# Attention's extra work spread over the steps, with two PSUM banks for row maxima and the division moved to GpSimd

## The chip, the cores and the metric

The kernel runs on one core of one Trainium2 chip. The metric is the device time of one execution in microseconds (us). Engines are named as in the profile: PE is TensorE, DVE is VectorE, ACT is ScalarE, POOL is GpSimd, SP issues most DMAs.

## What is computed

A chain of four blocks on x of shape (16, 64, 32, 32): a transformer block, a residual block of two 3x3 convolutions, an iterative whitening, and a state-space block. Only the attention of the first block is touched. It works on 16 images of 1024 positions, with 8 heads of 32 channels:

```python
x_ln = layer_norm(x_flat, g1, beta1)
qkv = x_ln @ w_qkv.T
q, k, v = jnp.split(qkv, 3, axis=-1)
scores = jnp.einsum('bhqd,bhkd->bhqk', q, k) * HEAD_DIM ** (-0.5)
attn = jax.nn.softmax(scores, axis=-1)
out = jnp.einsum('bhqk,bhkd->bhqd', attn, v)
```

All of it is float32 in the kernel, apart from bfloat16 copies of Q and K that serve only to find each row's maximum.

## The kernel before

Each phase of the kernel is a block of five instruction streams, one per engine, with semaphores between them. `attention_phase` takes the images one after another and the heads in two groups of four (`GH`), so there are 32 groups (`NG`). A group is one call of `period` in each engine's stream: 16 steps (`STEPS`), 8 for each half of 512 queries, each step one block of 128 keys. The first and the last group have stages of their own, a `lead` period runs ahead of the first, and the loop in `image_loop` covers four groups an iteration (two images), seven times.

In a step PE makes the transposed scores of four heads (`scores`, L398, one bank of `at_sc` each; a head uses 32 rows of the array) and takes off the maxima by a matmul with one row (`at_nrow`, L401). ACT takes the exponential of heads 0 and 1, then of heads 2 and 3 (L479), into `at_probs`; the scores of the next step wait for `exp_done` of the pair whose banks they use. PE multiplies the step before's `at_probs` by V (`values`, L410) into the bank `at_O`.

Beside this, the row maxima of the next group are made: in each step four matmuls of Q by K in bfloat16 (`maxima`, L334; heads 0 and 1 behind the scores, heads 2 and 3 at the step's end), each into one bank of `at_ring`, and DVE reduces each bank to 128 numbers (L526). `LATE` says how many of these maxima slip into the next period. Half of them are gathered by `combine`, turned by four matmuls with the identity (`turn`, L372) and copied by ACT into `at_nrow`.

The table `extra` puts the rest of the work in the steps: Q and K projections (`project`, L347, a matmul of 64 rows; ACT copies each to `at_QT` or `at_KT`, DVE casts it from the same bank to `at_QH` or `at_KH`, L542), V (`values_projected`, L360), the turns, and the softmax denominators (`denominators`, L385). POOL adds up five of the eight blocks of `at_probs` in four sums (L580); PE multiplies ones by the other three blocks and by that sum, which makes four terms of four heads into one bank. ACT makes the reciprocal of it as exp(-ln) in `at_lden` and `at_rden`, and DVE multiplies `at_O` by it (`normalise`, L549) into `at_att`, which SP stores. Values of a new half wait for that (`od_free`).

Maxima and extras share the three banks of `at_ring` in turn: `period_units` numbers them in the order in which PE issues them and gives each the number modulo `SLOTS`. `wait_for_bank` lets PE wait until the unit before it in the same bank was read, and for a projection also until it was cast.

## Time and profile before

| | us |
|---|---|
| median of 3 runs | 4073.43 (4072.83 to 4073.93) |
| the profiled execution | 4079.2 |
| its span, first to last instruction | 4077.5 |
| first exponential of attention (L479) starts | at 103.5 |
| last exponential of attention starts | at 2111.4 |
| busy: PE, DVE, ACT, POOL | 3426.7, 2982.9, 2143.2, 2103.6 |

Attention takes about half of the span. Everything is read from one profiled execution; its own time stands beside its span, and it is a little above the median of the runs. Busy time of PE counts matmuls whose ends are modelled, so starts are the better thing to read.

### The profile page before, as it was taken

The numbers are of one execution on the slowest core, as the hardware profiler recorded it, in microseconds if no ns is written. First come the engines' busy times: TensorE is split into PE (matmuls) and PEld (weight loads), VectorE is DVE, ScalarE is ACT, GpSimd is POOL, SyncE is SP. The second block draws the span as 40 slices with busy tenths as digits, with TensorE's granted clock in tenths as the row PEclk, the third lists the DMA queues.
The fourth block names the chain that finished last, engine by engine and source line by source line (L and its number), as shares of the span: only waits on it lengthen the run. The fifth ranks groups of instructions, "written<-read, shape, count | busy, mean of one in ns | idle before, by whom it ended". The sixth has DMA issues, their size and how long they took to land. (4 is left out here: it accounts for less than half of the span.)

```text
span 4077.5 us, 56384 instructions
## 1 busy us (share of the span) xinstructions
PE 3426.7 (84%) x19376; PEld 1233.0 (30%) x19376; DVE 2982.9 (73%) x3235; ACT 2143.2 (53%) x2331; POOL 2103.6 (52%) x586
## 2 busy tenths in 40 slices
PE   6999999999999999999978996567777777767766
PEld 2333333333333333333322333222222222222222
DVE  5677677676776767767722221489999999999999
ACT  3566566565665656656543332255555554555554
POOL 0556556565565555655660000156665666656665
PEclk7999999999999999999998998778888888888888
DMA  2000000000000000000013111200000000000000
GB/s 93 11 14 17 10 14 17 15 14 14 10 17 15 14 15 12 14 15 14 12 39 111 67 36 54 102 9 8 9 12 8 10 8 8 13 8 10 8 8 8
DMA packets 34702, 90.68 MB, mean 22 GB/s; under 512 B 8304, under 2 KB 9396, under 8 KB 34356
## 3 DMA queue, kind: packets, MB, share of 16 engines
q1 hardware_dynamic: 29396, 70.53, 5.6%
q0 software_dynamic: 5056, 16.83, 1.1%
q8 instruction: 155, 2.54, 0.3%
q14 instruction: 95, 0.78, 0.1%
HBM read 49.03 MB, written 38.27 MB: 21 GB/s over the span
## 5 line engine op out<-in xcount | busy, mean ns | idle before, releaser
L526 DVE TENSOR_REDUCE at_pmax<-at_ring 128x1 f32<-128x512 f32 x2048 | 1305.1, 685 | 511.4 <-PE at_ring L334 510.8
L479 ACT ACTIVATE at_probs<-at_sc 128x1024 f32<-128x1024 f32 x1024 | 992.5, 1021 | 659.6 <-PE at_sc L401 659.5
L1623 POOL TENSOR_TENSOR ss_drive<-ss_du,ss_bsb 128x1024 f32<-128x1024 f32 x261 | 865.2, 3333 | 392.4 <-ACT ss_bsb L1469 312.9
L580 POOL TENSOR_TENSOR at_prob_sums<-at_prob_sums,at_probs 128x2048 f32<-128x2048 f32 x192 | 869.4, 4528 | 109.8 <-ACT at_probs L479 98.7
L398 PE MATMUL at_sc<-at_QT,at_KT 32*128 32x512 f32 x4096 | 848.2, 643 | 21.3 <-issue 20.9
L1560 DVE TENSOR_TENSOR_SCAN ss_state<-ss_decay,ss_drive 128x1024 f32<-128x1024 f32 x259 | 774.7, 2991 | 7.5 <-ACT ss_decay L1476 5.1
L580 POOL TENSOR_TENSOR at_prob_sums<-at_probs 128x2048 f32<-128x2048 f32 x64 | 291.0, 4547 | 789.9 <-ACT at_probs L479 789.9
L1377 PE MATMUL ss_Y<-ss_seen,ss_ident 128*128 128x512 f32 x1032 | 598.3, 710 | 58.7 <-DVE ss_yv L1577 58.7
L410 PE MATMUL at_O<-at_probs,at_V 128*32 128x512 f32 x4096 | 538.9, 610 | 53.0 <-DVE at_att L549 51.8
L1469 ACT ACTIVATE ss_bsb<-ss_B 128x1024 f32<-128x1024 f32 x262 | 268.3, 1024 | 537.1 <-PE ss_B L1359 535.9
L334 PE MATMUL at_ring<-at_KH,at_QH 32*128 32x512 bf16 x2048 | 447.3, 389 | 5.7 <-DVE at_pmax L526 2.9
L1359 PE MATMUL ss_C<-ss_bc,ss_select 96*128 96x512 bf16 x518 | 175.5, 424 | 298.3 <-DVE ss_seen L1568 298.2
L401 PE MATMUL at_sc<-at_nrow,at_ones_bf 1*128 1x512 bf16 x2048 | 339.6, 381 | 0.0
L398 PEld LDWEIGHTS at_sc<-at_QT,at_KT 32*128 32x128 f32 x4096 | 275.1, 186 | 175.6 <-ACT at_probs L479 149.2
L1377 PEld LDWEIGHTS ss_Y<-ss_seen,ss_ident 128*128 128x128 f32 x1032 | 229.8, 227 | 315.0 <-issue 220.4
L1568 DVE TENSOR_TENSOR ss_seen<-ss_state,ss_C 128x1024 f32<-128x1024 f32 x259 | 316.2, 1221 | 9.5 <-DVE ss_state L1560 0.7
L334 PEld LDWEIGHTS at_ring<-at_KH,at_QH 32*128 32x128 bf16 x2048 | 150.9, 92 | 534.0 <-DVE at_pmax L526 343.0
L1476 ACT ACTIVATE ss_decay<-ss_delta,ss_a 128x1024 f32<-128x1024 f32 x261 | 297.4, 1140 | 2.9 <-DVE ss_delta L1544 2.9
L938 POOL DMA_DIRECT2D scratch_x<-fc_out x8 | 4.3, 536 | 351.5 <-ACT fc_out L839 351.5
L1359 PE MATMUL ss_B<-ss_bc,ss_select 96*128 96x512 bf16 x524 | 168.5, 405 | 13.3 <-ACT ss_bsb L1469 7.8
L385 PE MATMUL at_ring<-at_probs,at_ones 128*32 128x512 f32 x1512 | 175.3, 596 | 1.4 <-DVE at_pmax L526 1.4
L410 PEld LDWEIGHTS at_O<-at_probs,at_V 128*32 128x32 f32 x4096 | 87.5, 108 | 273.0 <-issue 189.1
(192 smaller groups left out, 2846.2 us busy)
## 6 DMA issues: line engine op xcount, KB each, us to landing
scratch_attn<-at_att SPq DMA_DIRECT2D x64, 256.0 KB, 2.0
fc_att<-scratch_attn SPq DMA_DIRECT2D x32, 512.0 KB, 5.8
at_xn<-scratch_xn SPq DMA_DIRECT2D x32, 256.0 KB, 3.8
ss_xn<-scratch_xm SPq DMA_DIRECT2D x17, 256.0 KB, 3.5
ss_xw<-scratch_xw SPq DMA_DIRECT2D x17, 256.0 KB, 3.4
ln_x<-in_x SPq DMA_DIRECT2D x8, 512.0 KB, 4.8
scratch_xn<-ln_xn POOLq DMA_DIRECT2D x8, 512.0 KB, 3.0
fc_x<-in_x SPq DMA_DIRECT2D x8, 512.0 KB, 7.7
```

Of the source, the lines that this page charges most:

```text
L334: nc.tensor.matmul(ring[:, unit[3], :], QH[head(h), p, blk(quad // 2)], KH[head(h), p, hs(quad % 2)], start=True, stop=True).then_inc(max_ ...
L398: nc.tensor.matmul(sc[:, h, :], KT[head(h), par, blk(kb)], QT[head(h), par, hs(half)], start=True, stop=False)
L401: m = nc.tensor.matmul(sc[:, h, :], ones_bf[row, :], nrow[row, half, :], start=False, stop=True)
L410: m = nc.tensor.matmul(O[head(h), :], V[:, par, kb, head(h)], probs[:, kb, h, :], start=(kb == 0), stop=(kb == KB - 1))
L479: nc.scalar.activation(probs[:, kb, two, :].rearrange("p h q -> p (h q)"), sc[:, two, :].rearrange("p h q -> p (h q)"), ACT.Exp, scale=SCA ...
L526: nc.vector.tensor_reduce(pmax[:, quad // 2, h, quad % 2:quad % 2 + 1], ring[:, unit[3], :], AX_X, ALU.max, negate=True).then_inc(max_done, 1)
L580: nc.gpsimd.tensor_tensor(prob_sums[:, half, :, :], before, probs[:, k, :, :], ALU.add).then_inc(pool_sums, 1)
L1359: m = nc.tensor.matmul(dst[:, hs(h)], select[:, first + n, :], bc[0:3 * 2 * N, par, hs(h)], start=True, stop=True)
L1377: m = nc.tensor.matmul(Y[:, hs(h)], ident[:], seen[:, n % DEPTH, hs(h)], start=(n == 0), stop=(n == N - 1))
L1560: nc.vector.tensor_tensor_scan(state[:, n % 2, :], decay[:, n % DEPTH, :], drive[:, n % DEPTH, :], 0.0, ALU.mult, ALU.add).then_inc(state_ ...
L1568: nc.vector.tensor_tensor(seen[:, n % DEPTH, :], state[:, n % 2, :], Cp[:], ALU.mult).then_inc(seen_done, 1)
L1623: nc.gpsimd.tensor_tensor(drive[:, n % DEPTH, :], du[:, par, :], bsb[:, n % DEPTH, :], ALU.mult).then_inc(drive_done, 1)
```

## The change

`LATE` goes from 3 to 5. Maxima get two banks, heads 0 and 2 the first and heads 1 and 3 the second; every extra goes to the third. The extras have one kind a step: Q, K, Q, K in steps 0 to 3, the turns in 6 and 14, V in halves in 7 and 8. The denominators of the second half of the group before are made in steps 4 and 5, two terms each, those of the first half in steps 10 to 13, one term each (`den_terms`), and values follow in every step. DVE casts a projection at the start of the next step. ACT copies `at_O` to the new tile `at_raw` (`take_out`) when a half's values are done; that frees `at_O`, and POOL multiplies the copy by the reciprocal after its sums of a half, under a new semaphore `att_done` that SP's store and ACT's next reciprocal wait for.

```diff
-    LATE = 3
+    LATE = 5
...
-    extra = {0: [("q", 0), ("k", 0)], 1: [("q", 1), ("k", 1), ("den", 1)], 4: [("turn", 1)], 6: [("v", 0), ("v", 1)],
-             9: [("den", 0)], 12: [("turn", 0)]}
+    extra = {0: [("q", 0)], 1: [("k", 0)], 2: [("q", 1)], 3: [("k", 1)], 5: [("den", 1)], 6: [("turn", 1)],
+             7: [("v", 0)], 8: [("v", 1)], 13: [("den", 0)], 14: [("turn", 0)]}
+
+    den_terms = {4: (1, (0, 1)), 5: (1, (2, 3)), 10: (0, (0,)), 11: (0, (1,)), 12: (0, (2,)), 13: (0, (3,))}
...
-        found, at = [], 0
+        found = []
         for s in range(STEPS):
-            plan = [("max", h) for h in (0, 1)] + extra.get(s, []) + [("max", h) for h in (2, 3)]
-            for kind, which in plan:
-                if executed(stage, kind, which, s):
-                    found.append((s, kind, which, at % SLOTS))
-                at += 1
+            plan = [("max", h) for h in range(GH)] + extra.get(s, [])
+            found += [(s, kind, which, which % 2 if kind == "max" else 2) for kind, which in plan
+                      if executed(stage, kind, which, s)]
...
                 srcs = [probs[:, k, :, :] for k in range(SUMMED + 1, KB)] + [prob_sums[:, half, :, :]]
-                for n, src in enumerate(srcs):
+                for n in terms:
+                    if n == 0:
+                        wait_for_bank(stage, grp, unit)
+                    if n == len(srcs) - 1:
+                        pe.wait_ge(pool_sums, SUMMED * (2 * (grp - half) + half + 1))
                     for h in range(GH):
-                        m = nc.tensor.matmul(ring[head(h), unit[3], :], ones[:, head(h)], src[:, h, :],
+                        m = nc.tensor.matmul(ring[head(h), unit[3], :], ones[:, head(h)], srcs[n][:, h, :],
                                              start=(n == 0), stop=(n == len(srcs) - 1))
...
+                    for kind, which in extra.get(s, []):
+                        if kind in "qk":
+                            project(stage, grp, par, kind, which)
+                        elif kind == "v":
+                            values_projected(stage, grp, par, which)
+                        elif kind == "turn":
+                            turn(stage, grp, which)
                     if stage != "lead":
-                        if s == 0:
-                            if stage != "first":
-                                values(grp - 1, 1 - par, STEPS - 1)
-                        elif s % KB == 2:
-                            values(grp, par, s - 2)
-                            values(grp, par, s - 1)
-                        elif s % KB != 1:
-                            values(grp, par, s - 1)
+                        if s in den_terms:
+                            denominators(stage, grp, *den_terms[s])
+                        if s:
+                            values(grp, par, s - 1)
+                        elif stage != "first":
+                            values(grp - 1, 1 - par, STEPS - 1)
...
+            def take_out(grp, half):
+
+                act.wait_ge(pv_done, STEPS * grp + KB * (half + 1))
+                if not (isinstance(grp, int) and grp == 0):
+                    act.wait_ge(att_done, 2 * grp + half - 1)
+                nc.scalar.activation(raw[:, half, :], O[:], ACT.Copy).then_inc(od_free, 1)
...
-                    if s == 2 and stage not in ("lead", "first"):
-                        normalise(grp - 1, 1)
-                    if s == KB + 2 and stage != "lead":
-                        normalise(grp, 0)
+                    for kind, which in extra.get(s - 1, []):
+                        if kind in "qk":
+                            cast(stage, grp, par, kind, which)
                     reduce(stage, grp, s, (0, 1))
-                    if s < 2:
-                        cast(stage, grp, par, s)
                     reduce(stage, grp, s, (2, 3))
...
         def _(pool):
+            def normalise(grp, half):
+                pool.wait_ge(rden_done, 2 * grp + half + 1)
+                pool.wait_ge(od_free, 2 * grp + half + 1)
+                if not (isinstance(grp, int) and grp == 0):
+                    pool.wait_ge(att_stored[half], grp * DMA)
+                nc.gpsimd.tensor_tensor(att[:, half, :], rden[:], raw[:, half, :], ALU.mult).then_inc(att_done, 1)
...
+                    if not (stage == "first" and half == 0):
+                        normalise(grp - 1 + half, 1 - half)
```

The order on PE around the denominators of the first half. Before, in step 9 (`at_ring<-at_KH,at_QH` is a matmul for maxima, `at_ring<-at_probs,at_ones` one for denominators, `at_sc` the scores):

```order
L334 MATMUL at_ring<-at_KH,at_QH 128x512 [waits at_max_done] x2
L385 MATMUL at_ring<-at_probs,at_ones 32x512 [waits at_pool_sums,at_max_done]
L385 MATMUL at_ring<-at_probs,at_ones 32x512 x11
L385 MATMUL at_ring<-at_prob_sums,at_ones 32x512 x4
L334 MATMUL at_ring<-at_KH,at_QH 128x512 [waits at_max_done] x2
L398 MATMUL at_sc<-at_QT,at_KT 128x512 [waits at_exp_done]
L398 MATMUL at_sc<-at_QT,at_KT 128x512
L398 MATMUL at_sc<-at_QT,at_KT 128x512 [waits at_exp_done]
L398 MATMUL at_sc<-at_QT,at_KT 128x512
L401 MATMUL at_sc<-at_nrow,at_ones_bf 128x512 x4
L334 MATMUL at_ring<-at_KH,at_QH 128x512 [waits at_extra_done]
L334 MATMUL at_ring<-at_KH,at_QH 128x512 [waits at_max_done]
```

Now, steps 10 and 11, from the maxima of heads 2 and 3 on:

```order
L335 MATMUL at_ring<-at_KH,at_QH 128x512 [waits at_max_done] x2
L385 MATMUL at_ring<-at_probs,at_ones 32x512 x4
L411 MATMUL at_O<-at_probs,at_V 32x512 x4
L335 MATMUL at_ring<-at_KH,at_QH 128x512 [waits at_max_done] x2
L399 MATMUL at_sc<-at_QT,at_KT 128x512 [waits at_exp_done]
L399 MATMUL at_sc<-at_QT,at_KT 128x512
L399 MATMUL at_sc<-at_QT,at_KT 128x512 [waits at_exp_done]
L399 MATMUL at_sc<-at_QT,at_KT 128x512
L402 MATMUL at_sc<-at_nrow,at_ones_bf 128x512 x4
L335 MATMUL at_ring<-at_KH,at_QH 128x512 [waits at_max_done] x2
```

All sixteen denominator matmuls stood together, and no values with them; now four stand ahead of the values of each step, between the maxima of heads 0 and 1 and those of heads 2 and 3.

The order on DVE in steps 0 to 3, where projections are cast. Before, from ahead of step 0's first cast (the rows of `at_pmax` are the reductions of the maxima):

```order
L526 TENSOR_REDUCE at_pmax<-at_ring 128x1 [waits at_max_ready] x22
L542 CAST at_QH<-at_ring 128x512 [waits at_extra_done]
L542 CAST at_KH<-at_ring 128x512 [waits at_extra_done]
L526 TENSOR_REDUCE at_pmax<-at_ring 128x1 [waits at_max_ready] x4
L542 CAST at_QH<-at_ring 128x512 [waits at_extra_done]
L542 CAST at_KH<-at_ring 128x512 [waits at_extra_done]
L526 TENSOR_REDUCE at_pmax<-at_ring 128x1 [waits at_max_ready] x6
L534 TENSOR_REDUCE at_negm<-at_pmax 128x16 [waits at_max_done]
```

Now:

```order
L534 TENSOR_REDUCE at_pmax<-at_ring 128x1 [waits at_max_ready] x16
L550 CAST at_QH<-at_ring 128x512 [waits at_extra_done]
L534 TENSOR_REDUCE at_pmax<-at_ring 128x1 [waits at_max_ready] x4
L550 CAST at_KH<-at_ring 128x512 [waits at_extra_done]
L534 TENSOR_REDUCE at_pmax<-at_ring 128x1 [waits at_max_ready] x4
L550 CAST at_QH<-at_ring 128x512 [waits at_extra_done]
L534 TENSOR_REDUCE at_pmax<-at_ring 128x1 [waits at_max_ready] x4
L550 CAST at_KH<-at_ring 128x512 [waits at_extra_done]
L534 TENSOR_REDUCE at_pmax<-at_ring 128x1 [waits at_max_ready] x4
L542 TENSOR_REDUCE at_negm<-at_pmax 128x16 [waits at_max_done]
```

Casts came in pairs between a step's second and third reduction; now there is one behind each step's fourth. DVE's multiplication into `at_att` is gone.

## Rows read from the trace of the kernel before

**Rows 1.** the page: busy time of each engine, two groups of POOL (busy us, mean ns)
```profile
PE 3426.7 (84%) x19376; PEld 1233.0 (30%) x19376; DVE 2982.9 (73%) x3235; ACT 2143.2 (53%) x2331; POOL 2103.6 (52%) x586
...
L1623 POOL TENSOR_TENSOR ss_drive<-ss_du,ss_bsb 128x1024 f32<-128x1024 f32 x261 | 865.2, 3333 | 392.4 <-ACT ss_bsb L1469 312.9
L580 POOL TENSOR_TENSOR at_prob_sums<-at_prob_sums,at_probs 128x2048 f32<-128x2048 f32 x192 | 869.4, 4528 | 109.8 <-ACT at_probs L479 98.7
```

**Rows 2.** windows: stretch and its us, then per engine busy us (instructions), PEclk, DMA
```profile
1050.14:1111.60 61.46, 58.85 (x483) 20.90 (x480) 44.59 (x72) 37.37 (x45) 36.24 (x8) 1.00 0.03 10
1238.59:1302.52 63.93, 61.46 (x484) 21.52 (x480) 44.86 (x72) 37.58 (x44) 36.27 (x8) 0.95 0.06 18
1238.59:1245.50 6.91, 6.91 (x30) 2.34 (x28) 3.91 (x6) 3.13 (x4) 0.00 (x0) 0.53 0.00 0
```

**Rows 3.** timeline at the loop's end: start, us, engine, line, instructions [idle before <-releaser]
```profile
1236.06 2.24 PE L398 MATMUL at_sc<-at_QT,at_KT 32*128 32x512 f32 x8 [3.26 <-issue]
...
1245.73 1.02 ACT L479 ACTIVATE at_probs<-at_sc 128x1024 f32<-128x1024 f32 x1 [3.27 <-PE at_sc L401]
```

**Rows 4.** timeline of ACT in the group from 1173.05
```profile
1173.05 1.94 ACT L479 ACTIVATE at_probs<-at_sc 128x1024 f32<-128x1024 f32 x2 [1.24 <-PE at_sc L401]
...
1177.72 1.94 ACT L479 ACTIVATE at_probs<-at_sc 128x1024 f32<-128x1024 f32 x2 [1.76 <-PE at_sc L401]
...
1188.94 1.94 ACT L479 ACTIVATE at_probs<-at_sc 128x1024 f32<-128x1024 f32 x2 [2.31 <-PE at_sc L401]
...
1198.48 1.94 ACT L479 ACTIVATE at_probs<-at_sc 128x1024 f32<-128x1024 f32 x2 [1.24 <-PE at_sc L401]
...
1206.12 1.94 ACT L479 ACTIVATE at_probs<-at_sc 128x1024 f32<-128x1024 f32 x2 [1.24 <-PE at_sc L401]
1209.30 1.94 ACT L479 ACTIVATE at_probs<-at_sc 128x1024 f32<-128x1024 f32 x2 [1.24 <-PE at_sc L401]
...
1218.59 1.94 ACT L479 ACTIVATE at_probs<-at_sc 128x1024 f32<-128x1024 f32 x2 [2.31 <-PE at_sc L401]
```

**Rows 5.** timeline of PE in a plain step
```profile
1206.20 1.07 PE L410 MATMUL at_O<-at_probs,at_V 128*32 128x512 f32 x8
...
1207.20 0.39 PE L334 MATMUL at_ring<-at_KH,at_QH 32*128 32x512 bf16 x2
```

**Rows 6.** timeline of step 10
```profile
1215.35 1.92 PE L410 MATMUL at_O<-at_probs,at_V 128*32 128x512 f32 x16 [0.82 <-DVE at_att L549]
...
1217.20 0.39 PE L334 MATMUL at_ring<-at_KH,at_QH 32*128 32x512 bf16 x2
...
1217.21 1.24 PE L398 MATMUL at_sc<-at_QT,at_KT 32*128 32x512 f32 x8
1217.63 1.29 DVE L526 TENSOR_REDUCE at_pmax<-at_ring 128x1 f32<-128x512 f32 x2 [1.14 <-PE at_ring L334]
...
1218.39 0.38 PE L334 MATMUL at_ring<-at_KH,at_QH 32*128 32x512 bf16 x2
...
1218.70 1.07 PE L410 MATMUL at_O<-at_probs,at_V 128*32 128x512 f32 x8
```

**Rows 7.** timeline of step 0
```profile
1173.28 1.29 DVE L526 TENSOR_REDUCE at_pmax<-at_ring 128x1 f32<-128x512 f32 x2 [0.61 <-PE at_ring L334]
1174.02 0.29 PEld L347 LDWEIGHTS at_ring<-at_xn,at_w 64*128 64x128 f32 x2 [0.59 <-DVE at_pmax L526]
1174.87 0.60 ACT L461 ACTIVATE at_QT<-at_ring 128x512 f32<-128x512 f32 x1
...
1175.08 1.06 PE L410 MATMUL at_O<-at_probs,at_V 128*32 128x512 f32 x8
...
1175.51 0.69 DVE L542 CAST at_QH<-at_ring 128x512 bf16<-128x512 f32 x1 [0.94 <-ACT at_QT L461]
```

**Rows 8.** timeline of step 6, PE
```profile
1199.46 1.16 PE L360 MATMUL at_ring<-at_w,at_xn 64*128 64x128 f32 x16 [0.82 <-DVE at_pmax L526]
```

**Rows 9.** timeline of step 4, PE
```profile
1192.20 0.40 PE L372 MATMUL at_ring<-at_ident,at_negm 128*128 128x128 bf16 x4
```

More of the change, by code:

```diff
@@ L284, in store @@
             def store(b, g, half):
-                sp.wait_ge(od_free, 2 * (GROUPS * b + g) + half + 1)
+                sp.wait_ge(att_done, 2 * (GROUPS * b + g) + half + 1)
                 sp.dma_start(attn_d[bass.ds(b, 1), g * P:(g + 1) * P, hs(half)].rearrange("a c s -> (a c) s"),
@@ L350, in values_projected @@
-            def values_projected(stage, grp, par):
-                if not executed(stage, "v", 0, 6):
-                    return
-                units = [unit_of(stage, "v", n) for n in range(2)]
-                for unit in units:
-                    wait_for_bank(stage, grp, unit)
-                at = 2 * INNER + (1 - par) * P
-                for k in range(KB):
-                    n = k % 2
-                    rows = slice(n * C, (n + 1) * C)
-                    m = nc.tensor.matmul(ring[:, units[n][3], blk(k // 2)], xn[rows, blk(k)], w[rows, at:at + P],
+                unit = unit_of(stage, kind, half)
@@ new lines, in project, with values_projected @@
+                wait_for_bank(stage, grp, unit)
+                n = "qk".index(kind)
+                rows = slice(n * C, (n + 1) * C)
+                at = n * INNER + (1 - par) * P
+                nc.tensor.matmul(ring[:, unit[3], :], w[rows, at:at + P], xn[rows, hs(half)],
+                                 start=True, stop=True).then_inc(extra_ready, 1)
+            def values_projected(stage, grp, par, n):
+                if not executed(stage, "v", n, 0):
+                    return
+                unit = unit_of(stage, "v", n)
+                wait_for_bank(stage, grp, unit)
+                at = 2 * INNER + (1 - par) * P
+                for j in range(KB // 2):
+                    rows = slice(n * C, (n + 1) * C)
+                    m = nc.tensor.matmul(ring[:, unit[3], blk(j)], xn[rows, blk(2 * j + n)], w[rows, at:at + P],
@@ L374, in turn, with denominators @@
                 m.then_inc(extra_ready, 1)
-            def denominators(stage, grp, half):
+            def denominators(stage, grp, half, terms):
                 if not executed(stage, "den", half, 0):
@@ L481, in period @@
                                                  scale=SCALE).then_inc(exp_done, 1)
+                    if kb == 0 and stage not in ("lead", "first") or stage == "first" and s == KB:
+                        take_out(grp - 1 + half, 1 - half)
                     for kind, which in extra.get(s, []):
```

61 lines of the change are left out of this document (21 added, 40 removed).

## The prediction, made before the change was timed

> **What bounds the kernel now.** I first read the page [rows 1]: TensorE is busy 84% of the span and no other engine is above 73%. The page's queue and DMA lines show nothing near full, so I went to one attention group. The windows view cut at group boundaries [rows 2] gives 61.46 us for a plain group, with TensorE busy 58.85 of it (96%) and granted its full clock; DVE is busy 44.59, ACT 37.37 and POOL 36.24. Attention is 32 such groups and only it is changed. One boundary in four (the loop's end) costs more: TensorE idles 3.26 us without a releaser [rows 3], and the group behind it takes 63.93 at a mean granted clock of 0.95 [rows 2]. Nothing in the change touches that.
>
> The ACT timeline of a group [rows 4] gives its steps: a step is the time from one pair of exponentials to the next. A step with nothing extra takes 3.18 us (1209.30 - 1206.12). Step 0 takes 4.67, 1.49 more; steps 1 and 2 together 11.22, 4.86 more; steps 6 and 7 together 7.64, 1.28 more (V); steps 9 and 10 together 9.29, 2.93 more. That is 10.56, and with 16 x 3.18 the group. These lumps are what the change spreads out.
>
> **A plain step** is a loop of two engines [rows 4, 5]: ACT works 1.94, then idles 1.24 until the scores are back, because heads 2 and 3 wait for the second exponential. **A step full of TensorE work** runs differently [rows 6], step 10 with two `values` of four heads: values start at 1215.35, max matmuls of heads 2 and 3 at 1217.20 with the scores of all four heads right behind (the exponentials were long done), the exponential at 1218.59 [rows 4], the next values at 1218.70. So from the max matmuls M to the next exponential is 1.39, to the next full-array work 1.50, and a step without waits is 3.35 with two values. From one set of values to M is 1.00 (1206.20 to 1207.20), from two sets 1.85: one set costs 0.85, and so does a denominator term, which has the same shape. A step with only its own values would be 3.35 - 0.85 = 2.50 of work: 0.68 of each plain step is free.
>
> **The change, part by part**, for a middle group; X is the extra TensorE work of a step.
> - Denominators: four terms as one burst (steps 1, 9) become two terms in steps 4 and 5, and one each in 10 to 13. Same matmuls; X = 1.70 or 0.85.
> - Projections: Q and K in steps 0 and 1 become one each in steps 0 to 3. The K matmul starts at 1174.02 and values follow at 1175.08 [rows 7]: X = 1.05. The two V halves, 1.16 together [rows 8], now go one a step, each on 64 of the array's rows. The bounds are 0.58 and 1.16; I take 1.0, since on different rows the two halves most likely ran side by side, as the heads' scores do.
> - Turns: X = 0.40 [rows 9], in steps 6 and 14.
> - Output: DVE's two multiplications leave (0.69 each, by its cast of the same shape [rows 7]); ACT adds a copy of 0.60 (as its Q copy [rows 7]) after the values of steps 0 and 8, POOL a multiplication. The values at the start of a half no longer wait for a reciprocal (0.82 at 1215.35 [rows 6]). For POOL's price the bounds are DVE's 0.69 and half of its own 128x1024 multiply, 3.33 / 2 = 1.67 [rows 1]; I take 1.2, a quarter of its 4.53 for 128x2048 [rows 1] plus a little. POOL is idle 25 us of a group [rows 2]. Its four sums of half 0 (18.1 us from step 1) end in step 5, and the reciprocal of step 13 asks for that product much later, so it costs nothing in the loop; if POOL were full, ACT's reciprocal would wait for `att_done` with every exponential behind it. The Trainium skill (GPSIMD Engine Reference, section 4.1) says to keep elementwise work of two inputs on VectorE since GpSimd takes about twice as long. My 1.2 against 0.69 agrees with that. Were the difference on the path in each of 64 halves, it would be +33 us, 4183; by the rows POOL has room and it is 0.
> - ACT in step 0: values end about 2.4 after the step's start, copy 0.6, Q 0.6: 3.6 to 3.9, under the 4.02 below. Close, but hidden; the same in step 8. If its cover went, each would cost its excess over the step. SP's stores wait for `att_done` and nothing waits for SP.
>
> **The banks are the price.** Maxima now have two banks, so head 1's max matmul of a step needs the reduction of head 3 of the step before; with three banks it needed head 2's. Heads 2 and 3 are issued at M = 1217.20 [rows 6], DVE starts at 1217.63, needs 1.29 for both (done at M + 1.71), and the release takes about 0.05 (1173.28 + 0.69 to 1174.02 [rows 7]): head 1 can start at M + 1.77. Before, it started at M + 1.19 (1218.39), on time. TensorE works in order, so extras and values stand behind it, and from such a matmul to full-array work is 0.31 (1218.39 to 1218.70). So they start at M + 2.07, not M + 1.50. To the next M is X + 1.00 (values 1206.20, M 1207.20 [rows 5]). **A step in a row of full steps takes 3.07 + X**; in place of 2.50 + X. The DVE work that was free is now inside the chain.
>
> In steps 1 to 4 there is more: the third bank holds one extra at a time, released by DVE's cast, which stands behind head 3's reduction. Reductions start 0.61 apart (1.29 for two, the last 0.69): cast at M + 0.42 + 1.22, done 0.69 later, released M + 2.38. Steps 1 to 3 take 2.38 + 1.05 + 1.00 = 4.43.
>
> The sum of a group, each step in us: step 0 4.02 (behind a plain step whose M is 1.69 after its exponential: M + 1.77 is 0.27 into step 0, + 0.31 + 1.05 + 1.00 + 1.39); 1 to 3 13.29; 4 2.38 + 1.70 + 1.00 = 5.08; 5 4.77; 6 3.47; 7 and 8 8.14; 9 3.18 (its chain needs only 3.07); 10 3.82; 11 to 13 11.76; 14 3.47; 15 3.18. Total 64.18 against 61.46: **+2.72 per middle group, 30 groups: +82.** It is a gain of 10.56, all lumps gone, and a loss of 13.3 in new ones.
>
> At the ends: the first group has no steps 4/5 denominators (about -1.5 by the same table); the last has no projections, and two more steps of maxima are hidden in it: about 4 less; copy and POOL's product add 1 at the end; the lead-in reduces 8 maxima fewer (-5) and loses as much to cast chains and to two banks at half clock. Together -5, from rows only roughly. The profiled execution (4079.2, span 4077.5) gives 4079 + 77 = 4156; it is 5.8 above the median of the runs, 4073.43, to which I apply the sum: **4150**.
>
> **Rivals.**
> A, faster: the banks never delay TensorE. It needs M to head 1's matmul to last 1.77 by itself, as when heads 2 and 3 still wait for the exponential [rows 4, 5], or max matmuls not blocking what is behind. Steps are then 3.18 or 2.50 + X: 4 x 3.55 + 2 x 4.20 + 2 x 3.50 + 4 x 3.35 + 4 x 3.18 = 55.7, so -5.74 x 30 - 5 = -177: 3896. For it: DVE is idle 27% of a group and loses two multiplications. Against: full steps have M so late that scores of all heads overlap [rows 6], which is just when 1.19 is left. Chance 0.12. The Trainium skill (PSUM — Partial Sum Buffer, Engine vs sequencer instructions) says matmuls start and complete in program order, which speaks against it; the K matmul that waited for DVE with the values behind it [rows 7] shows the same.
> B, half of the price: the maxima wait costs little (0.21 for 0.31 behind it, V cheaper), or the cast wait does not show: -1.2 each per group, 4114 for one of them, 4078 for both. It is the low side of my main case and shares its chance.
> C, slower yet: TensorE's many short idle stretches cost it the clock. After the idle time of 3.26 step 0 took 7.14 (1238.59 to 1245.73 [rows 2, 3]) in place of 4.67 at a granted clock of 0.53 [rows 2], near the 1.2 GHz level. One such fall per group is +2.47 x 30 = +74: 4224. The Trainium skill (TensorE: Matmul & The Clock Gate, A second HAM failure mode) describes matmul groups cycling through PSUM banks with small idles that make the clock go up and down. Against: the longest new idle is about 0.9, and a plain group, whose values wait 0.82 (rows 6), has a granted clock of 1.00 [rows 2]. Chance 0.08.
> D: ring and spread cancel (price half as large in all steps), 4065 to 4082 after the ends: 0.05.
>
> **Numbers.** Main case 0.75, A 0.12, C 0.08, D 0.05. The range reaches from B's corner, 4078, less a few us for the ends, to the costs I may have missed above (ACT's copy showing 0.2 twice a group, +12; each of six split projections 0.1 more, +18; the ends, +5): 4185. A measurement of this kernel can tell about 0.2% (8 us) from no change. Faster 0.15, same 0.05, slower 0.80.
>
> **What would show it.** Right: plain group 64.1; steps 1 to 3 near 4.4, 11 to 13 near 3.9, 9 and 15 at 3.18; TensorE idle before `at_ring` max matmuls or what stands behind them, released by DVE `at_pmax`; DVE idle longer. Wrong: steps 11 to 13 at 3.35 (A); granted clock under 1.00 in plain groups (C); ACT waiting for POOL `at_att`; head 1's max matmul issued less than 1.7 after heads 2 and 3.

## The result, and the profile after

The changed kernel takes 4179.12 us (median of 4 runs, 4171.41 to 4185.2) against 4073.68 of the kernel before (4 runs, 4072.83 to 4075.81). The ratio is 1.0257 [1.0239, 1.0275], slower by 105 us. The forecast was 4150, range 4075 to 4185. The profiled execution of after took 4177.0 (span 4175.3) at the same mean granted clock as before, 0.914.

The page of the kernel after, with the busy time of each engine and two groups of instructions (busy us, mean ns, idle time of the engine ahead of them and what ended it):

```profile
PE 3479.0 (83%) x19376; PEld 1247.1 (30%) x19376; DVE 2925.0 (70%) x3171; ACT 2187.7 (52%) x2395; POOL 2182.1 (52%) x650
...
L534 DVE TENSOR_REDUCE at_pmax<-at_ring 128x1 f32<-128x512 f32 x2048 | 1295.5, 684 | 728.4 <-PE at_ring L335 725.7
```

TensorE has the same 19376 matmuls as before [rows 1], DVE 64 instructions fewer, and both idle more. The waits view of after says who stood for whom (us in all, times, longest):

```profile
ACT at_probs L484 <- PE at_sc L402: 749.4, 508, 6.7
DVE at_pmax L534 <- PE at_ring L335: 725.7, 521, 5.6
PEld at_ring L335 <- DVE at_pmax L534: 665.6, 1254, 1.5
```

The last row, weight loads of max matmuls waiting for a reduction, is the one to read. Before, it was half of that:

```profile
PEld at_ring L334 <- DVE at_pmax L526: 343.0, 442, 1.3
```

Three rows of this sort rise together (ACT behind the scores 749.4, 659.5 before; DVE behind the max matmuls 725.7, 510.8 before): everybody waits for somebody, which is what a loop through three engines looks like.

Windows of after: a plain group, the next one with a loop's end in it, and a group behind another loop's end (columns as in rows 2):

```profile
896.41:960.74 64.33, 60.35 (x487) 21.23 (x480) 42.71 (x71) 38.85 (x46) 38.74 (x10) 1.00 0.06 18
960.84:1030.37 69.53, 61.78 (x484) 21.50 (x481) 42.92 (x71) 38.86 (x47) 38.76 (x10) 0.96 0.03 10
1294.45:1368.02 73.57, 71.37 (x485) 23.97 (x479) 42.76 (x70) 38.85 (x46) 38.69 (x10) 0.81 0.05 15
```

The plain group, at the full clock, took 64.33 for 61.46 before [rows 2]; 64.18 was forecast. ACT's timeline in it (start, duration, instructions, idle time before) gives the steps, as rows 4 did before:

```profile
896.51 1.94 ACT L484 ACTIVATE at_probs<-at_sc 128x1024 f32<-128x1024 f32 x2 [1.24 <-PE at_sc L402]
899.29 0.60 ACT L466 ACTIVATE at_raw<-at_O 128x512 f32<-128x512 f32 x1 [0.84 <-PE at_O L411]
899.79 0.59 ACT L459 ACTIVATE at_QT<-at_ring 128x512 f32<-128x512 f32 x1
900.55 1.94 ACT L484 ACTIVATE at_probs<-at_sc 128x1024 f32<-128x1024 f32 x2 [0.17 <-PE at_sc L402]
...
904.96 1.94 ACT L484 ACTIVATE at_probs<-at_sc 128x1024 f32<-128x1024 f32 x2 [1.68 <-PE at_sc L402]
...
942.43 1.94 ACT L484 ACTIVATE at_probs<-at_sc 128x1024 f32<-128x1024 f32 x2 [1.90 <-PE at_sc L402]
946.37 1.94 ACT L484 ACTIVATE at_probs<-at_sc 128x1024 f32<-128x1024 f32 x2 [2.00 <-PE at_sc L402]
```

Step 0 is 900.55 - 896.51 = 4.04, step 1 4.41, step 11 3.94. Over all 32 groups the medians of the starts, step by step, beside the forecast:

```
step      0    1    2    3    4    5    6    7    8    9    10   11   12   13   14   15
forecast  4.02 4.43 4.43 4.43 5.08 4.77 3.47 4.07 4.07 3.18 3.82 3.92 3.92 3.92 3.47 3.18
measured  4.03 4.41 4.41 4.42 5.08 4.80 3.41 4.17 4.17 3.18 3.84 3.94 3.94 3.94 3.41 3.18
```

The two round trips that make these numbers are both at the start of step 2 of that group (M is again the start of the max matmuls of heads 2 and 3). TensorE, then DVE:

```profile
902.57 1.06 PE L411 MATMUL at_O<-at_probs,at_V 128*32 128x512 f32 x8
903.57 0.39 PE L335 MATMUL at_ring<-at_KH,at_QH 32*128 32x512 bf16 x2
903.58 1.24 PE L399 MATMUL at_sc<-at_QT,at_KT 32*128 32x512 f32 x8
904.54 0.50 PE L402 MATMUL at_sc<-at_nrow,at_ones_bf 1*128 1x512 bf16 x4
904.76 0.37 PE L335 MATMUL at_ring<-at_KH,at_QH 32*128 32x512 bf16 x1
905.34 0.38 PE L335 MATMUL at_ring<-at_KH,at_QH 32*128 32x512 bf16 x1 [0.21 <-DVE at_pmax L534]
905.94 0.69 PE L348 MATMUL at_ring<-at_xn,at_w 64*128 64x512 f32 x1 [0.21 <-DVE at_KH L550]
```

```profile
903.99 1.29 DVE L534 TENSOR_REDUCE at_pmax<-at_ring 128x1 f32<-128x512 f32 x2 [1.33 <-PE at_ring L335]
905.20 0.68 DVE L550 CAST at_KH<-at_ring 128x512 bf16<-128x512 f32 x1
```

Heads 2 and 3 are issued at M = 903.57; DVE has both reduced at 905.28; head 1's matmul starts at 905.34 = M + 1.77. The projection behind it waits on for the cast (done 905.88) and starts at 905.94 = M + 2.37. Values and the next M follow in order. ACT's exponentials are not late for any reason of their own; their scores are.

**Where the time went**, on the profiled executions (+97.8):

```
first exponential starts at 111.34, before 103.55             +7.8
first group 63.1, before 65.5                                  -2.4
30 middle groups, 64.33 - 61.46 = 2.87 each                   +86.1
the same groups, longer stretches of low clock                 +8.8
last group                                                     -5.2
from the last exponential's start to the end                   +2.7
```

The fourth line is the rest of the middle groups beyond 30 x 2.87. The last line is not shown to be a price of the change: this stretch, which holds little of attention, differs by up to 10 among the profiles of the experiments. Most of the fourth line is the third window above, 73.57 at a granted clock of 0.81. In its first steps ACT's timeline reads:

```profile
1294.55 1.94 ACT L484 ACTIVATE at_probs<-at_sc 128x1024 f32<-128x1024 f32 x2 [6.35 <-PE at_sc L402]
...
1301.28 1.94 ACT L484 ACTIVATE at_probs<-at_sc 128x1024 f32<-128x1024 f32 x2 [1.25 <-PE at_sc L402]
...
1308.02 1.94 ACT L484 ACTIVATE at_probs<-at_sc 128x1024 f32<-128x1024 f32 x2 [3.71 <-PE at_sc L402]
```

Steps of 6.73 at a granted clock of 0.50: four in a row here, one or none behind the other five loop ends. Steps 1 to 3 of this group are 2.3 too long each, 7 of the 8.8; the rest is a little more at each loop end. The runs of after spread over 14 us, those of before over 3 here and over 5 to 12 beside the experiments.

### The profile page after: what moved, and what is told of

Its sections match the earlier page's. It is cut to its first block and busy times, and to the rows that moved or that the text cites. A ratio compares the mean times of both kernels' runs of the same rounds, so it can differ in the third digit from the quotient of the medians.

```text
span 4175.3 us, 56463 instructions
## 1 busy us (share of the span) xinstructions
PE 3479.0 (83%) x19376; PEld 1247.1 (30%) x19376; DVE 2925.0 (70%) x3171; ACT 2187.7 (52%) x2395; POOL 2182.1 (52%) x650
## 5 line engine op out<-in xcount | busy, mean ns | idle before, releaser
L534 DVE TENSOR_REDUCE at_pmax<-at_ring 128x1 f32<-128x512 f32 x2048 | 1295.5, 684 | 728.4 <-PE at_ring L335 725.7
L484 ACT ACTIVATE at_probs<-at_sc 128x1024 f32<-128x1024 f32 x1024 | 992.7, 1021 | 752.3 <-PE at_sc L402 749.4
L399 PE MATMUL at_sc<-at_QT,at_KT 32*128 32x512 f32 x4096 | 665.8, 632 | 22.8 <-issue 22.7
L335 PE MATMUL at_ring<-at_KH,at_QH 32*128 32x512 bf16 x2048 | 600.9, 393 | 100.6 <-DVE at_pmax L534 92.2
L411 PE MATMUL at_O<-at_probs,at_V 128*32 128x512 f32 x4096 | 549.6, 609 | 0.9 <-ACT at_probs L484 0.9
L335 PEld LDWEIGHTS at_ring<-at_KH,at_QH 32*128 32x128 bf16 x2048 | 142.5, 91 | 899.1 <-DVE at_pmax L534 665.6
L402 PE MATMUL at_sc<-at_nrow,at_ones_bf 1*128 1x512 bf16 x2048 | 270.7, 383 | 0.0
L399 PEld LDWEIGHTS at_sc<-at_QT,at_KT 32*128 32x128 f32 x4096 | 227.1, 187 | 37.7 <-issue 25.4
L385 PE MATMUL at_ring<-at_probs,at_ones 128*32 128x512 f32 x1512 | 195.2, 603 | 6.3 <-DVE at_KH L550 6.3
L348 PE MATMUL at_ring<-at_xn,at_w 64*128 64x512 f32 x256 | 157.5, 698 | 42.9 <-DMA at_xn<-scratch_xn 19.3
```

Source lines behind the costliest of these rows:

```text
L335: nc.tensor.matmul(ring[:, unit[3], :], QH[head(h), p, blk(quad // 2)], KH[head(h), p, hs(quad % 2)], start=True, stop=True).then_inc(max_ ...
L399: nc.tensor.matmul(sc[:, h, :], KT[head(h), par, blk(kb)], QT[head(h), par, hs(half)], start=True, stop=False)
L411: m = nc.tensor.matmul(O[head(h), :], V[:, par, kb, head(h)], probs[:, kb, h, :], start=(kb == 0), stop=(kb == KB - 1))
L484: nc.scalar.activation(probs[:, kb, two, :].rearrange("p h q -> p (h q)"), sc[:, two, :].rearrange("p h q -> p (h q)"), ACT.Exp, scale=SCA ...
L534: nc.vector.tensor_reduce(pmax[:, quad // 2, h, quad % 2:quad % 2 + 1], ring[:, unit[3], :], AX_X, ALU.max, negate=True).then_inc(max_done, 1)
```

## The experiments

Times are medians of 4 runs (6 for f4), each with its ratio to the kernel before on the same chip and the 95% interval. That kernel took 4074.71, 4076.19 and 4079.6 us beside the first four, the next four, and g1 and the h kernels. "Group" is a plain middle group at full clock. The theory is that the bank rule (two banks, head 1 waits for head 3's reduction) and the cast wait are the price; the rivals put it into the spreading of the denominators, the early output or the clock. Kernels measured beside different times of before are best compared by their ratios.

**Without the cast wait, casts from the SBUF copy.** The projection's bank is released by ACT alone; DVE casts from `at_QT`/`at_KT`:

```diff
-                    if before[2][1] in "qk":
-                        pe.wait_ge(cast_done, casts(before[1], *before[2][1:3]))
...
-                to = QH if kind == "q" else KH
-                nc.vector.tensor_copy(to[:, 1 - par, hs(which)], ring[:, unit[3], :]).then_inc(cast_done, 1)
+                to, src = (QH, QT) if kind == "q" else (KH, KT)
+                nc.vector.tensor_copy(to[:, 1 - par, hs(which)], src[:, 1 - par, hs(which)]).then_inc(cast_done, 1)
```

> The changed kernel with one edit: DVE casts Q and K from ACT's copy in SBUF, so the extras' bank is free as soon as ACT has copied it. Theory (banks): the M + 2.38 of steps 1 to 4 becomes M + 2.07 as in other full steps, so steps 1, 2, 3 fall from 4.41 to 4.13 and step 4 from 5.08 to 4.79; a middle group 63.1 in place of 64.33, the time 36 us less, about 4143. Rival (the splitting itself costs: projections no longer side by side, more switches between kinds of matmul, ACT's copy): the bank wait was covered, steps 1 to 4 stay within 0.05, the time stays at 4179 +- 8.

Measured: 4193.6, 1.0303 [1.0286, 1.032], not faster but 14 slower than after. Step 1 fell from 4.41 to 4.13 as expected; steps 2 and 3 rose to 5.43 and 4.65. DVE and POOL in those steps:

```profile
907.82 0.42 DVE L547 CAST at_QH<-at_QT 128x512 bf16<-128x512 f32 x1
...
911.95 2.46 DVE L547 CAST at_KH<-at_KT 128x512 bf16<-128x512 f32 x1
914.33 2.47 DVE L531 TENSOR_REDUCE at_pmax<-at_ring 128x1 f32<-128x512 f32 x4
916.72 2.33 DVE L547 CAST at_QH<-at_QT 128x512 bf16<-128x512 f32 x1
```

```profile
909.59 4.53 POOL L579 TENSOR_TENSOR at_prob_sums<-at_probs 128x2048 f32<-128x2048 f32 x1 [9.85 <-ACT at_probs L481]
914.20 4.57 POOL L579 TENSOR_TENSOR at_prob_sums<-at_prob_sums,at_probs 128x2048 f32<-128x2048 f32 x1
```

The cast takes 0.42 with POOL idle. Started inside a sum of POOL's it ends 0.29 after that sum does (911.95 + 2.46 = 914.41, the sum ends 914.12), and again (919.05 and 918.77). All 93 casts of this trace that start inside a sum end 0.28 or 0.29 after it, and take 0.8 to 3.0 by how early in the sum they start. The reductions from PSUM beside the same sums keep their 0.6. So this removed one wait and set up another; it says nothing against the theory and is no clean test of it. The Trainium skill (SBUF — State Buffer, Who interferes with whom) describes it: a copy or cast of DVE whose operands meet the conditions of a two-port mode takes the port pair that DVE shares with GpSimd, an exclusive lock for a whole instruction, while a DVE instruction with at most one SBUF input outside these modes does not contend. These rows agree, with 2.46 beside a sum, 0.42 without one, and 0.6 a reduction beside a sum.

**Denominators as bursts again, on top of that**, in steps 4 and 12:

```diff
...
-    den_terms = {4: (1, (0, 1)), 5: (1, (2, 3)), 10: (0, (0,)), 11: (0, (1,)), 12: (0, (2,)), 13: (0, (3,))}
+    den_terms = {4: (1, (0, 1, 2, 3)), 12: (0, (0, 1, 2, 3))}
```

> e1 with the four denominator terms of a half in one step again (steps 4 and 12, with values in the same step), maxima still on two banks. Theory: a full step costs 3.07 + X once in place of several times, but its free 0.11 to 0.68 is used once too: step 12 about 6.2, step 4 about 6.5 (3.07 + 3.42), steps 5, 10, 11, 13 at 3.18; group 62.9, time within 10 us of e1, about 4138. Rival (spreading is what pays, as the change means it): 2 to 3 us a group more than e1, 4200 or above.

Measured: 4186.05, 1.0283 [1.0266, 1.03]; group 64.43 for e1's 64.62. Where the terms stand hardly matters. The level is off by e1's casts.

**Three banks in turn, on top of that:** the numbering of before comes back (max 0, 1, extras, max 2, 3, each the next number modulo 3).

> e2 with one edit: maxima and extras take the three banks in turn, as in the kernel before. Theory (banks): the wait of head 1's max matmul for head 3's reduction goes where M is late; step 12 falls to about 5.9, steps 0 to 3 to 3.5 to 3.8, step 4 to 6.2, steps 7 and 8 to 3.5 and 3.8, all others 3.18; group about 59.8, 3.1 less than e2, time about 4045 and so faster than before. Rival (the splitting or GpSimd's multiplication costs, not the banks): within 10 us of e2.

Measured: 4168.24, 1.0239 [1.0218, 1.0261], with middle groups from 62 to 72 and a mean granted clock of 0.896. Step 0 fell to 3.52, 7 and 8 to 3.56 and 3.85, 5 and 6 to 3.18, all as expected. The time was missed by 120: steps 2 and 3, expected at 3.5 to 3.8, stayed in the casts' trouble (medians 5.75 and 6.16), and of the 18 middle groups away from the loop ends 16 were granted less than the full clock. One of them in the windows view:

```profile
228.20:294.44 66.24, 64.46 (x482) 22.83 (x480) 46.96 (x70) 38.69 (x46) 38.77 (x10) 0.92 0.05 17
```

TensorE's longest idle time in this group is 1.17 (at 239.21, ahead of a max matmul that waits for reductions behind a cast of 2.77), where it is 0.21 in the plain group of after and 0.83 in that of before, both granted 1.00. So this is what rival C describes, in another kernel than the one it was made for. Inconclusive on the price, so the banks were tried again below.

**Only the early output, on the kernel before:** `take_out` on ACT at the end of its steps 0 (behind the Q and K copies) and 8, POOL's multiplication behind its sums, nothing else.

```diff
-                nc.vector.tensor_tensor(att[:, half, :], rden[:], O[:], ALU.mult).then_inc(od_free, 1)
...
+                nc.scalar.activation(raw[:, half, :], O[:], ACT.Copy).then_inc(od_free, 1)
...
+                nc.gpsimd.tensor_tensor(att[:, half, :], rden[:], raw[:, half, :], ALU.mult).then_inc(att_done, 1)
```

> The kernel before with one part of the change: ACT copies the output out in steps 0 and 8 (behind the projections' copies) and POOL multiplies. Steps, banks and denominators as before. Theory: the values of steps 2 and 10 no longer wait 0.82 for DVE's product; steps 2 and 10 fall from 4.24 to about 3.35, group 59.7 in place of 61.45, time 4020. POOL's product takes about 1.2 and ends long before it is asked for. Rival (the output part costs: ACT's copy delays exponentials, or POOL's product delays its sums and ACT's exponentials that wait for them): steps 0, 8 or 9 grow by 0.5 or more and the gain is under half, 4050 or more.

Measured: 4025.05, 0.9872 [0.9856, 0.9889]. Its plain group in the windows view:

```profile
840.18:899.85 59.67, 58.71 (x483) 20.89 (x480) 43.31 (x70) 38.45 (x47) 38.72 (x10) 1.00 0.06 19
```

1.79 less than before, 54 us in 30 groups; steps 2 and 10 fell from 4.24 to 3.36, as expected. That part of the change is a gain, and it was hidden in the whole.

**ACT makes the bfloat16 copies, on the changed kernel:** ACT copies a projection twice from PSUM, DVE's casts and the wait for them go, `take_out` moves behind the extras.

```diff
                         if kind in "qk":
+                            act.wait_ge(extra_ready, unit_count(stage, grp, unit))
+                            nc.scalar.activation({"q": QH, "k": KH}[kind][:, 1 - par, hs(which)], ring[:, unit[3], :],
+                                                 ACT.Copy).then_inc(cast_done, 1)
...
-                        if kind in "qk":
-                            cast(stage, grp, par, kind, which)
```

> The changed kernel, with Q and K in bfloat16 written by ACT from PSUM (a second copy of 0.60) in place of DVE's cast; the extras' bank is free after both copies; ACT's copy of the output comes behind them. This is e1's question without a cast from SBUF. Theory (DVE's cast behind head 3's reduction held the bank): steps 1, 2, 3 at 4.13 and step 4 at 4.79 in place of 4.41 and 5.08, group 63.15, with a shorter lead-in about 4139. Rival (e1 was slow because casts never mattered and something else in steps 2 to 4 grows once they are gone): steps 2 and 3 again above 4.6, 4180 or more.

Measured: 4128.17, 1.0121 [1.0102, 1.0139], group 63.19. Steps 1 to 3 are 4.13 each (4.41), step 4 4.80 (5.08), the rest unchanged. This is what e1 was to be. 51 us less than after, 34 of them from the plain groups (30 x 1.14); by the profiles the lead-in gives 2 and the groups at loop ends 10, most of it because this profile has no long stretch of low clock.

**The same with the denominators as bursts:** e2's edit on f1.

> f1 with the four denominator terms in one step (4 and 12), two banks for maxima. Theory: steps 4 and 12 near 6.3 and 6.2, steps 5, 6, 13, 14 near 3.25, group 63.2, about 4140, the same as f1. Rival (spreading the denominators pays by itself): 60 us or more slower than f1.

Measured: 4134.78, 1.0145 [1.0124, 1.0166], group 63.20. Step 4 takes 6.51 and 5 and 6 3.27 and 3.22, where f1 had 4.80, 4.80 and 3.41: 13.00 against 13.01. One term a step is worth nothing under this bank rule, because a step in which the chain through DVE is full has no free time to put a term into.

**The same with three banks in turn:** e3's edit on f2.

```diff
-            plan = [("max", h) for h in range(GH)] + extra.get(s, [])
-            found += [(s, kind, which, which % 2 if kind == "max" else 2) for kind, which in plan
-                      if executed(stage, kind, which, s)]
+            plan = [("max", h) for h in (0, 1)] + extra.get(s, []) + [("max", h) for h in (2, 3)]
+            for kind, which in plan:
+                if executed(stage, kind, which, s):
+                    found.append((s, kind, which, at % SLOTS))
+                at += 1
```

> f2 with one edit: maxima and extras take three banks in turn as in the kernel before. Theory (two banks for maxima are the price of the change): steps 0 3.52, 1 to 3 3.82, 4 about 6.2, 7 3.56, 8 3.85, 12 5.90, all others 3.18; group 59.9, lead-in 10 us shorter as between e2 and e3, about 4035: 100 us less than f2 and faster than before. Rival (banks matter little; splitting and GpSimd cost): within 20 us of f2.

Measured: 4028.86, 0.9894 [0.9867, 0.992]. Between f2 and f3 only the bank of each unit differs: 106 us. Their plain groups, f2 first:

```profile
881.38:944.58 63.20, 60.84 (x483) 22.16 (x480) 40.66 (x67) 40.61 (x51) 38.72 (x10) 1.00 0.06 18
```

```profile
832.23:892.16 59.93, 58.94 (x483) 21.77 (x480) 40.64 (x66) 40.44 (x50) 38.71 (x10) 1.00 0.06 19
```

TensorE at the start of step 2 of f3, as in the rows of after above:

```profile
838.18 0.39 PE L334 MATMUL at_ring<-at_KH,at_QH 32*128 32x512 bf16 x2
838.18 1.24 PE L398 MATMUL at_sc<-at_QT,at_KT 32*128 32x512 f32 x8
839.15 0.50 PE L401 MATMUL at_sc<-at_nrow,at_ones_bf 1*128 1x512 bf16 x4
839.37 0.38 PE L334 MATMUL at_ring<-at_KH,at_QH 32*128 32x512 bf16 x2
839.95 1.12 PE L347 MATMUL at_ring<-at_xn,at_w 64*128 64x512 f32 x2 [0.20 <-DVE at_pmax L536]
```

Heads 0 and 1 are together at M + 1.19 (M = 838.18) and the extra waits for head 3's reduction, M + 1.77: the wait is still there, but the 0.31 from a max matmul to full-array work is paid before it, not behind it, so this step is 3.82 for 4.13. In a step with no extra nothing needs that bank so early, and the steps behind the bursts fall from 3.27 and 3.22 to 3.18. The group saves 3.27 (98 us in 30), and the first exponential comes 11.7 earlier (97.65 for 109.35).

**Head 1's max matmul behind the extra**, on f1 in the steps of denominators and V, so that only values stand behind its wait:

```diff
-                    maxima(stage, grp, par, s, (0, 1))
+                    apart = s in den_terms or s in (7, 8)
+                    maxima(stage, grp, par, s, (0,) if apart else (0, 1))
...
+                    if apart:
+                        maxima(stage, grp, par, s, (1,))
```

> f1 with one edit on TensorE's order, banks untouched: in steps with denominator terms or V, head 1's max matmul stands behind the extra work and ahead of the values, so that its wait for head 3's reduction is over before TensorE gets there. Theory: a full step becomes 2.50 + X plus one more change between kinds of matmul (0.31) in place of 3.07 + X: steps 4 and 5 from 4.8 to 4.5, 7 and 8 from 4.17 to 3.9, 10 to 13 from 3.84 to 3.94 to 3.67; group 2.1 less than f1, 62 us less than f1, about 4077. Rival (the wait is hidden and the steps are long because of the work in them): steps 0.3 longer by the extra change of kind, 70 us more than f1.

Measured: 4103.94, 1.0063 [1.0044, 1.0082], group 61.91 for 63.19. The gain is 24 us, under half of what was expected; the plain groups give 38 (30 x 1.28), and this profile has one group of 73.0 behind a loop's end, at half clock. V's steps fell as expected (4.17 to 3.89), the denominators' by 0.14 and not 0.27. TensorE in step 11, with one denominator term:

```profile
919.36 0.38 PE L332 MATMUL at_ring<-at_KH,at_QH 32*128 32x512 bf16 x1
919.67 1.06 PE L382 MATMUL at_ring<-at_probs,at_ones 128*32 128x512 f32 x8
920.67 0.38 PE L332 MATMUL at_ring<-at_KH,at_QH 32*128 32x512 bf16 x1
920.98 1.06 PE L408 MATMUL at_O<-at_probs,at_V 128*32 128x512 f32 x8
```

The wait is gone, as the theory has it. But a set of full-array matmuls that runs into others costs 0.85, and here it takes 1.00 to the max matmul and 0.31 from there to the values: 1.31, so 0.46 for a max matmul on its own in the middle. The expectation had the 0.31 and not the 0.15 ahead of it.

**e4 with DVE multiplying the copy** in steps 2 and 10, from SBUF, and not POOL:

```diff
-                nc.gpsimd.tensor_tensor(att[:, half, :], rden[:], raw[:, half, :], ALU.mult).then_inc(att_done, 1)
+                nc.vector.tensor_tensor(att[:, half, :], rden[:], raw[:, half, :], ALU.mult).then_inc(att_done, 1)
```

> e4 with one edit: DVE multiplies ACT's copy (in SBUF) by the reciprocal in steps 2 and 10, in place of POOL. In e1 a DVE cast from SBUF took 0.42 alone and 2.3 to 2.7 while POOL worked on a sum. Theory (such a DVE instruction waits for POOL's to end): the multiplication of step 2 and that of step 10, where POOL is in a sum, take 1 to 4.5 in place of 0.69 and hold up the maxima behind them; 1 to 3 us more in each of steps 2 and 10, 4085 to 4205. Rival (the cast's slowness is of its own kind, a multiplication is not touched): 0.69 is hidden, the time within 10 us of e4's 4025.

Measured: 4053.56, 0.9938 [0.9922, 0.9955], 28 above e4. The tile view of `at_att` (count, duration in ns min/median/max, first and last start), g1 and then e4:

```profile
L559 DVE TENSOR_TENSOR at_att<-at_rden,at_raw x64: 681/1139/2001, 149.3 to 2093.6; 128x512 f32<-128x512 f32 x64
```

```profile
L575 POOL TENSOR_TENSOR at_att<-at_rden,at_raw x64: 1253/1273/1294, 164.5 to 2067.2; 128x512 f32<-128x512 f32 x64
```

Step 10 rose from 3.35 to 4.21, step 2 did not, the group from 59.67 to 60.52. The two products of one group, in steps 2 and 10, tell why:

```profile
242.78 0.68 DVE L559 TENSOR_TENSOR at_att<-at_rden,at_raw 128x512 f32<-128x512 f32 x1
271.54 1.83 DVE L559 TENSOR_TENSOR at_att<-at_rden,at_raw 128x512 f32<-128x512 f32 x1
```

The first falls between two sums of POOL's (one ends at 242.14, the next starts at 244.65), the second into one (268.27 to 272.82) and ends 0.55 after it. So it is in all 64: 0.68 or 0.69 outside a sum, 1.59 to 2.00 inside one. The effect is there, in one of the two steps alone, and the time is below the expected range; POOL's steady 1.27, which nobody waits for, is the better place.

**e4 with V in halves**, in steps 6 and 8 (each half its own unit, as in the changed kernel).

> e4 with one edit of the change's splitting: V in halves, in steps 6 and 8, banks in turn. Theory (with three banks in turn a single full step costs 2.50 + X): steps 6 and 8 about 3.55 each in place of 4.45 and 3.18, 0.5 us a group less, about 4010. Rival (splitting costs: X is 1.09 for both halves together and 1.0 for each alone): V in halves costs 0.3 or more a group, 4034 or above.

Measured: 4017.85, 0.9847 [0.9831, 0.9863]. Steps 6 and 8 are 3.56 each, as expected, but step 9, the denominators' burst, grew from 5.05 to 5.42; the group is 59.52 for 59.67, a gain of 0.15 for the 0.5 expected. The burst of one group:

```profile
262.81 2.78 PE L383 MATMUL at_ring<-at_probs,at_ones 128*32 128x512 f32 x24 [0.28 <-DVE at_pmax L533]
```

It takes the bank of head 3's maxima, as in f3, and the half of V has made step 8 full, so that M is late (260.96) and the burst waits until M + 1.85. In e4, where step 8 is plain, it starts without a wait. It is the bank wait again, with three banks.

**f3 with values doubled behind the bursts:** no values in steps 4 and 12, two sets in 5 and 13.

```diff
-                        if s:
+                        if s and (s - 1) in den_terms:
+                            values(grp, par, s - 2)
+                        if s and s not in den_terms:
                             values(grp, par, s - 1)
...
```

> f3 with one edit: no values in the steps of the denominators (4, 12), two sets in the step behind (5, 13), as in the kernel before. Theory: a burst leaves no free time to use, so its own values are better made in the step behind, which has 0.68 free: 6.20 + 3.18 becomes 5.35 + 3.36 and 5.90 + 3.18 becomes 5.05 + 3.36; group 58.6 in place of 59.94, 40 us less than f3, about 3989. Rival (only the sum of TensorE's work counts): the same as f3 within 10 us.

Measured: **3990.22**, 0.9778 [0.9761, 0.9794], faster than both kernels and the lowest median here. Its group:

```profile
820.98:879.82 58.84, 57.10 (x483) 21.12 (x480) 40.51 (x66) 40.31 (x50) 38.76 (x10) 1.00 0.07 19
```

Step 4 fell from 6.20 to 5.34 and 12 from 5.90 to 5.05; steps 5 and 13, with two sets, are 3.36. A burst without values leaves the next step enough free time for them. It was expected at 58.6 a group; step 7 rose from 3.56 to 3.83. Step 5 with its two sets is full, so the turn behind it waits 0.27 for head 3's reduction, the next M comes late (846.42), and the half of V waits too, until M + 1.77 (848.19). In f3 neither waits.

**h2 with V's second half in step 9:**

> h2 with the second half of V in step 9 in place of 8. Theory: with three banks the loss of 0.29 in step 8 comes from the full step ahead of it (7); apart, both take 3.56, 0.3 a group less, 9 us less than h2. Rival: no difference beyond 5 us.

Measured: 3996.93, 0.9798 [0.9779, 0.9817]. The group is 58.55, 0.3 less as expected (step 9 takes 3.56 and step 8 3.18, where h2 had 3.18 and 3.85; step 7 stays at 3.83, not 3.56), yet the time is the same within the intervals: this profile has one group of 70.7 behind a loop's end, at half clock.

## Why the prediction was right

**Whole.** 2.87 a group for 2.72, slower by 105 for 77. The mechanism and the sum of a plain group are right. The median is only 6 us under the upper bound of the range, though, and the bound was set for other costs: ACT's copy showed nowhere, of the six split projections only the two of V took more, and the clock, which did cost, had no term. That the ends and the clock fell inside the range is in part luck. The experiments take the 2.87 apart, in plain groups, as a chain from before over e4, f3, f2 and f1 to after (so that the sum must come out, and each price holds beside the parts that were there): early output -1.79 (e4 for before), extras spread, five late maxima and ACT's bfloat16 together +0.26 (f3 for e4), the bank rule +3.27 (f2 for f3), denominators as terms -0.01 (f1 for f2, on two banks), the cast wait +1.14 (after for f1). The sum is +2.87.

**The banks.** "A step in a row of full steps takes 3.07 + X": steps 10 to 14 and 4 to 8 came out within 0.1 with X from the rows, M + 1.77 is in the timeline, and undoing only the numbering (f3 for f2) gave 106 us back.

**The cast chain**, release at M + 2.38 and steps of 4.43: 2.37 and 4.41. Without it 4.13 (f1).

**The early output.** It was rightly put down as hidden, ACT's copy at 0.60 and POOL's product at 1.27 for a taken 1.2 (0.68 on DVE, in g1). The 33 us that it would cost on the path are not there; e4 shows that all of it is gain, and g1 that DVE would have been the worse place with both inputs in SBUF (28 us).

**Rivals.** A (3896, the banks never delay) fell in f3 against f2. B (a price half as large) fell in every full step, and the cast wait alone is 1.14. C (one fall of the clock in each group, 4224) did not come here, a plain group is granted 1.00; it came in e3, with longer idle times, and here in small, as most of the 9 us, behind one loop end. D fell with B.

**Mis-sized terms of the sum**, which leave 98 on the profiled executions where 77 was forecast:

- The ends, "together -5, from rows only roughly": +2.9. The first group gave -2.4 for -1.5, the last -5.2 for "about 4 less", and behind them +2.7 for "1" (a stretch that varies more than that from profile to profile). The miss is the lead-in, which came out at +7.8 where "-5" and "loses as much" made it 0. It runs at half clock, granted 0.50 in both kernels. Its two-bank part was right, since each pair of maxima waits for the pair before:

```profile
96.76 1.21 PE L335 MATMUL at_ring<-at_KH,at_QH 32*128 32x512 bf16 x2 [0.18 <-DVE at_pmax L534]
98.15 1.22 PE L335 MATMUL at_ring<-at_KH,at_QH 32*128 32x512 bf16 x2 [0.17 <-DVE at_pmax L534]
```

  That is 1.39 for two maxima, 0.69 each, where before DVE reduced 20 in a row in 12.24, 0.61 each. From the first max matmul to the first scores it takes 33.6 (75.22 to 108.80) with 44 maxima, before 33.3 (67.70 to 101.01) with 52. What was too small is the cast chain ahead of it. All four projections now take one bank, each behind the cast of the one before. After, the first, the second and the first max matmul behind all four:

```profile
61.06 2.04 PE L348 MATMUL at_ring<-at_xn,at_w 64*128 64x512 f32 x2 [19.28 <-DMA at_xn<-scratch_xn]
64.67 2.04 PE L348 MATMUL at_ring<-at_xn,at_w 64*128 64x512 f32 x2 [1.57 <-DVE at_QH L550]
75.22 0.61 PE L335 MATMUL at_ring<-at_KH,at_QH 32*128 32x512 bf16 x2 [1.41 <-DVE at_KH L550]
```

  Before, two projections went together, and the first max matmul came 7.7 behind the first of them:

```profile
60.03 2.08 PE L347 MATMUL at_ring<-at_xn,at_w 64*128 64x512 f32 x4 [19.29 <-DMA at_xn<-scratch_xn]
67.70 0.71 PE L334 MATMUL at_ring<-at_KH,at_QH 32*128 32x512 bf16 x3 [1.42 <-DVE at_KH L542]
```

  14.2 for 7.7 is 6.5 of the 7.8; 1.0 is that attention started later in this profile. Three banks took 10.6 us off the lead-in in e3 (for e2) and 11.7 in f3 (for f2).
- X of half a V: 1.0 taken, 1.10 measured (4.17 - 3.07). The two halves, 1.16 together [rows 8], ran side by side nearly in full, as argued, and even more so. +6 in 30 groups.
- The turn: 0.40 taken, 0.34 measured. -4.
- The clock: no term was there, and of the loop's end the prediction said that nothing in the change touches it; +9. What decides whether the low clock behind a loop's end lasts one step or four stays open. One such stretch stands in each of the profiles of after, e1, e2, e3, f4 and h3, none in those of before, e4, f1, f2, f3, g1, h1 and h2.

## What to carry to other kernels

For buffers used in turn, count from the last write of one round to the first write that needs it back, through the reader: here M + 1.77 against a need at M + 1.19. A wait on an engine that works in order is paid by all that stands behind it, so a separate pool of banks for the rarer work made every full step longer, with no work added.

Free time in a step (0.68 of each plain one) is only there to be filled if the buffers don't tie that step to the one before; test a spreading with the ring as it was. No run here has the denominators spread with three banks in turn, so what the spreading by itself would be worth stays open. And a change of several parts should be timed in parts: this one held a 50 us gain under a 150 us loss, and the version that keeps the gain, leaves three banks in turn, takes the cast off DVE, makes the denominators in bursts again and puts their values into the step behind (h2) is 2.2% faster than before.

## What the runs showed of the hardware

- **A cast of DVE from SBUF to SBUF**, 128x512 float32 to bfloat16, took 0.42 with POOL idle and 0.8 to 3.0 when it started inside a sum of POOL's with two inputs, ending 0.28 to 0.29 after it (e1). From PSUM the same cast took 0.68 to 0.69 in after, inside a sum or not. The product of two float32 tiles in SBUF took 0.68 outside a sum and 1.59 to 2.00 inside, ending 0.55 after it (g1). Neither was expected when e1 was designed.
- **A max matmul between full-array sets** costs 0.46: 0.15 ahead of it and 0.31 behind (f4).
- **Half the clock for four steps.** After the idle stretch at a loop's end (3.26 [rows 3], 3.66 ahead of the third window of after) TensorE ran at the lower level for one step in the kernel before, at all its loop ends. In six profiles (after, e1, e2, e3, f4, h3) it did so once each for four steps of 6.73, and for one or two, or part of one, at their other loop ends. e3 and h3 have three banks in turn, so the bank rule alone isn't the reason.
- **Falls of the clock inside the loop.** In e3, with idle times of TensorE up to 1.17 in a group, 16 of 18 groups away from loop ends were granted less than 1.00; before and after, with at most 0.83 and 0.21, were granted 1.00 there.
